# A graph layer on one core: the order of the table's chunks and the raw rows, and a first ring round worked off group by group

## The reference

```python
h = jnp.maximum(_layernorm(x, axis=-1), 0.0)                   # eps 1e-5
msg_in = jnp.concatenate([h[senders], edges], axis=-1)         # 320 values
agg = jax.ops.segment_sum(msg_in @ W_message, receivers, num_segments=12500)
g = _layer_norm(jax.nn.relu(agg) + h, ln_aggr_scale, ln_aggr_bias)
y = _relu_mlp_skip(g, [W0, W1, W2], [b0, b1, b2])              # three 256x256 layers
out = x + _layer_norm(h + y, ln_out_scale, ln_out_bias)
```

## Time and profile before

| | |
|---|---|
| median of 3 runs | 2189.6 us |
| profiled execution | 2189.61 us, span 2187.8 us |
| POOL busy | 1598.8 us, 73% |
| PE busy | 1700.8 us, 78% |
| DVE, ACT busy | 960.6 us, 393.6 us |
| first gather from the table | 133.80 us after the span's start |
| last gather issued | 2150.81 us |

### The profile page before, as it was taken

One profiled execution on the slowest core, in us unless ns is written; L12 is line 12 of the kernel. 1 busy time (PEld: TensorE's weight loads), 2 busy tenths in 40 slices (PEclk: granted clock), 3 DMA queues, 4 the chain that ended last, 5 costly groups with the idle time before them and its releaser, 6 DMA issues.

```text
span 2187.8 us, 31761 instructions
## 1 busy us (share of the span) xinstructions
PE 1700.8 (78%) x6728; PEld 1142.8 (52%) x6729; DVE 960.6 (44%) x4123; ACT 393.6 (18%) x1185; POOL 1598.8 (73%) x1672
## 2 busy tenths in 40 slices
PE   0149987888888788888788788878878878878887
PEld 0137765555555455555555555545545555545555
DVE  8956544344343434344343434434343434333345
ACT  2942111111111111111111111111111111111112
POOL 7547777777777777777777777777777777777772
PEclk9779999989888989999899899999998998999988
DMA  9966655555555555555555555555555555555542
GB/s 326 328 211 178 174 160 156 149 159 161 147 160 146 156 154 158 151 159 161 149 156 152 153 155 159 158 151 154 153 158 151 159 148 160 151 159 148 157 136 57
DMA packets 360746, 356.47 MB, mean 163 GB/s; under 512 B 250048, under 2 KB 303360, under 8 KB 360704
## 3 DMA queue, kind: packets, MB, share of 16 engines
q0 software_dynamic: 79872, 218.21, 34.6%
q1 hardware_dynamic: 221504, 83.44, 14.6%
q10 hardware_dynamic: 59328, 54.36, 7.8%
HBM read 329.39 MB, written 26.48 MB: 163 GB/s over the span
## 4 chain that ended last, share of the span: by engine, by line
POOL 66%; issue 21%; PE 4%; ACT 3%; DMA 3%; DVE 2%; POOLq 0%; SPq 0%; DVEq 0%
POOL ring L344 66%; PE acc_banks L489 2%; ACT xs L619 2%; DMA ring<-h_table,src_all 2%; ACT ring L619 1%; DMA xs<-x 1%; PE agg_bank L394 0%; PE agg_bank L399 0%; DVE x_stats L859 0%; PE y_bank L382 0%; PE z_bank L382 0%; DMA h_table<-xs 0%; PE acc_banks L394 0%; PE acc_banks L497 0%; ACT x_std L611 0%
## 5 line engine op out<-in xcount | busy, mean ns | idle before, releaser
L344 POOL DMA_INDIRECT ring<-h_table,src_all x1600 | 1530.8, 957 | 527.6 <-issue 484.4
L489 PE MATMUL acc_banks<-ring,onehot 128*128 128x320 f32 x3328 | 1147.9, 494 | 419.8 <-DMA ring<-h_table,src_all 341.9
L489 PEld LDWEIGHTS acc_banks<-ring,onehot 128*128 128x128 f32 x3328 | 673.4, 213 | 847.3 <-issue 689.2
L956 DVE TENSOR_SCALAR onehot<-iota,dst_rel 128x128 f32<-128x128 f32 x1664 | 354.4, 300 | 1157.5 <-PE acc_banks L489 1122.7
L533 ACT ACTIVATE uT<-z_bank,fp 128x128 f32<-128x128 f32 x196 | 79.1, 453 | 963.2 <-PE z_bank L388 959.2
L394 PE MATMUL agg_bank<-wm,ST 128*128 128x256 f32 (+1 forms) x582 | 164.2, 403 | 0.0
L394 PEld LDWEIGHTS agg_bank<-wm,ST 128*128 128x128 f32 (+1 forms) x582 | 105.6, 194 | 55.2 <-issue 35.1
L399 PE MATMUL agg_bank<-wl,u 128*128 128x256 f32 x392 | 111.6, 407 | 0.0
L549 ACT ACTIVATE std<-mv,eps 128x2 f32<-128x2 f32 x97 | 28.7, 296 | 448.9 <-DVE mv L677 448.9
L539 ACT ACTIVATE r_bank<-y_bank,fp 128x128 f32<-128x128 f32 x196 | 58.7, 337 | 280.3 <-PE y_bank L382 280.3
L382 PEld LDWEIGHTS y_bank<-u,wl 128*128 128x128 f32 x784 | 102.9, 191 | 5.3 <-issue 0.3
(11 more groups left out here) (166 smaller groups left out, 1032.0 us busy)
## 6 DMA issues: line engine op xcount, KB each, us to landing
ring<-edges SPq DMA_DIRECT2D x208, 256.0 KB, 3.6
ring<-h_table,src_all POOLq DMA_INDIRECT x1600, 2.8
xs<-x SPq DMA_DIRECT2D x14, 896.0 KB, 10.0
h_table<-xs SPq DMA_DIRECT2D x14, 896.0 KB, 5.0
h_in<-h_table ACTq DMA_DIRECT2D x98, 128.0 KB, 2.4
visit_rows<-h_table ACTq DMA_DIRECT2D x98, 128.0 KB
visit_rows<-x ACTq DMA_DIRECT2D x98, 128.0 KB
out<-o ACTq DMA_DIRECT2D x93, 128.0 KB
```

Source lines behind the costliest of these rows:

```text
L344: nc.gpsimd.indirect_dma_start(out=ring[:, g % RG * G + j, 0:D], out_offset=None, in_=rows, in_offset=bass.IndirectOffsetOnAxis(ap=src_all ...
L489: return nc.tensor.matmul(acc_of(at), onehot[:, (k % OG) * G + j, :], ring[:, k * G + j, :], start=False, stop=True, skip_group_check=True)
L956: op = nc.vector.tensor_scalar(onehot[:, ((k + AHEAD) % OG) * G + j, :], iota[:, :], dst_rel[:, bass.ds((g + AHEAD) * G + j, 1)], None, AL ...
```

## The change

UNITS now is chunks 0 to 12, raw 0, chunk 13, raw 1 to raw 7. The first FIRST = 16 units (up to raw 1) are taken before the loop over groups. In `x_moments(u)` the aggregation of unit u-1 now comes behind the first statistics of unit u, and `x_stats` has two halves. Raw 2 to raw 7 are taken one at a time, between the first round's groups: on DVE `x_moments(16+k)` and then group k, on ACT `x_root` and `x_to_h` of raw k+1 and then group k's visit, if it has one. DVE's and ACT's first round is written out; DVE's loop starts at round 1 and ACT's loop at the visit that follows the first round. A second pass over the edges (for unusual edge lists, not taken here) now stands under an `If` on DVE. The first round's edge loads go out with chunks 6 to 13, not 0 to 7.

The key setup is shared out: ACT copies `blk` and `dst_f` and makes both range checks with a sum over the row (`accum_out`); DVE's two row-wide reductions, the product `blk * ok` and the cast of `blk` go; the remaining parts stand behind units 0, 1, 3, 4, 5 and 6, and the first one-hots in front of units 14 and 15.

```diff
-    UNITS = []
-    for n in range(NX):
-        UNITS.append(("chunk", n))
-        if 3 <= n < 3 + RG:
-            UNITS.append(("raw", n - 3))
-    UNITS += [("raw", k) for k in range(max(NX - 3, 0), RG)]
+
+
+    UNITS = [("chunk", n) for n in range(NX)]
+    UNITS.insert(NX - 1, ("raw", 0))
+    UNITS += [("raw", k) for k in range(1, RG)]
+    FIRST = NX + 2
...
-                if n < RG:
-                    load_edges(n, 0, n + 1)
+                if n >= NX - RG:
+                    load_edges(n - NX + RG, 0, n - NX + RG + 1)
                 if n >= 1 and n - 1 + XS < NX:
                     sp.wait_ge(h_stored[(n - 1) % XS], 16 * ((n - 1) // XS + 1))
                     load_x(n - 1 + XS)
...
+            act.wait_ge(lasts_ready, 1)
+            nc.scalar.activation(blk[:, 1:T + 1], last_i[:, :], ACT.Copy).then_inc(blocks_ready, 1)
             x_root(0)
-            for u in range(1, len(UNITS)):
+            act.wait_ge(dst_in, 16)
+            nc.scalar.activation(dst_f[:, :], dst_i[:, :], ACT.Copy).then_inc(dst_ready, 1)
+            for u in range(1, FIRST - 1):
                 x_root(u)
+                if u == 2:
+
+                    act.wait_ge(rel_ready, 1)
+                    nc.scalar.activation(rel[:, :], rel[:, :], ACT.Relu, bias=highest[:, 0:1],
+                                         accum_out=wrong[:, 0:1]).then_inc(wrong_ready, 1)
+                    nc.scalar.activation(below[:, :], below[:, :], ACT.Relu, scale=-1.0,
+                                         accum_out=wrong[:, 1:2]).then_inc(wrong_ready, 1)
                 x_to_h(u - 1)
-            x_to_h(len(UNITS) - 1)
+            x_to_h(FIRST - 2)
             act.wait_ge(params_in, PARAMS)
...
-            sel_reg = registers(nc.scalar, 1)
+            regs = registers(nc.scalar, W - AT)
+            before = [nc.scalar.alloc_register(f"before{k}") for k in range(4)]
 
             def row(b):
                 return out_blocks[:, bass.ds(b, 1), :].rearrange("p b d -> p (b d)")
 
-            for n in range(LAG):
-                sel = numbers(nc.scalar, sel_reg, visit_sel, n, 1)[0]
-                act_visit(act, n, sel, max(n - 1, 0), max(n - 4, 0), dump)
-            with nc.scalar.Fori(LAG, NB - 1) as n:
-                sel = numbers(nc.scalar, sel_reg, visit_sel, n, 1)[0]
-                act_visit(act, n, sel, n - 1, n - 4, row(n - LAG))
-            sel = numbers(nc.scalar, sel_reg, visit_sel, NB - 1, 1)[0]
+            def visit(n, sel):
+
+                load_at, late_at, store_at = (floored(nc.scalar, to, n, -lag) for to, lag in zip(before, (1, 4, LAG)))
+                act_visit(act, n, sel, load_at, late_at, row(store_at))
+
+
+            for k in range(RG):
+                if k + 1 < RG:
+                    x_root(FIRST - 1 + k)
+                    x_to_h(FIRST - 1 + k)
+                _, sel, closes, _ = numbers(nc.scalar, regs, steer_flat, k * W + AT, G - 1, 1, T)
+                n = floored(nc.scalar, before[3], regs[VISIT - AT])
+                with nc.scalar.If(closes > 0):
+                    visit(n, sel)
+                    nc.scalar.nop()
+            nc.scalar.load(regs[0:1], steer_flat[0:1, RG * W + VISIT:RG * W + VISIT + 1])
+            visited = floored(nc.scalar, before[3], regs[0])
+            with nc.scalar.Fori(visited, NB - 1) as n:
+                sel = numbers(nc.scalar, regs[1:2], visit_sel, n, 1)[0]
+                visit(n, sel)
+            sel = numbers(nc.scalar, regs[1:2], visit_sel, NB - 1, 1)[0]
             act_end(act, sel, row(NB - 1 - LAG))
...
+            def x_aggregate(u):
+                dve.wait_ge(x_stats_ready, u + 1)
+                if u >= 2:
+                    dve.wait_ge(x_norm_ready, u - 1)
+                for k in range(XB if UNITS[u][0] == "chunk" else G):
+                    op = nc.vector.bn_aggr(x_mv[:, u % 2, k, :], x_stats[:, u % 2, k, :])
+                op.then_inc(x_moments_ready, 1)
...
-                if u >= 1:
-                    dve.wait_ge(x_moments_ready, u)
+                if u >= 2:
+                    dve.wait_ge(x_moments_ready, u - 1)
+                left = [] if u == 0 else list(range(5))
                 for k in range(count):
                     rows_at = xs[:, n % XS, k, :] if kind == "chunk" else ring[:, n * G + k, 0:D]
-                    op = nc.vector.bn_stats(x_stats[:, k, :], rows_at)
+                    op = nc.vector.bn_stats(x_stats[:, u % 2, k, :], rows_at)
                     if k == count - 1:
                         op.then_inc(x_stats_ready, 1)
-                    if u >= 1 and k < 5:
-                        x_scale(u - 1, k)
-                dve.wait_ge(x_stats_ready, u + 1)
-                if u >= 2:
-                    dve.wait_ge(x_norm_ready, u - 1)
-                for k in range(count):
-                    op = nc.vector.bn_aggr(x_mv[:, u % 2, k, :], x_stats[:, k, :])
-                op.then_inc(x_moments_ready, 1)
-
...
+            def check_keys():
+                dve.wait_ge(blocks_ready, 1)
+                dve.wait_ge(dst_ready, 1)
+                nc.vector.scalar_tensor_tensor(rel[:, :], blk[:, 1:T + 1], -float(P), dst_f[:, :], ALU.mult, ALU.add)
+                nc.vector.scalar_tensor_tensor(below[:, :], blk[:, 0:T], -float(P), dst_f[:, :], ALU.mult, ALU.add).then_inc(rel_ready, 1)
+                step(nc.vector.tensor_tensor(spans[:, :], blk[:, G:T + 1:G], blk[:, 0:T:G], ALU.subtract))
+                step(nc.vector.tensor_reduce(widest[:, :], spans[:, :], AX.X, ALU.max))
+                nc.vector.tensor_scalar(narrow[:, :], widest[:, :], 1.0, None, ALU.is_le)
+
+            def relative_keys():
+                dve.wait_ge(wrong_counted, 1)
+                step(nc.vector.tensor_reduce(n_wrong[:, :], n_wrong_at, AX.X, ALU.add))
+                step(nc.vector.tensor_scalar(ok[:, :], n_wrong[:, :], 0.0, narrow[:, 0:1], ALU.is_equal, ALU.mult))
+                nc.vector.tensor_copy(ok_i[:, :], ok[:, :])
+                step(nc.vector.tensor_scalar(per_block[:, :], ok[:, :], -float(P), None, ALU.mult))
+                step(nc.vector.scalar_tensor_tensor(dst_rel[:, 0:T], blk[:, 1:T + 1], per_block[:, 0:1], dst_f[:, :], ALU.mult, ALU.add))
+                nc.vector.tensor_scalar(dst_rel[:, T:T + AHEAD * G], dst_rel[:, 0:AHEAD * G], -float(P), None, ALU.add).then_inc(keys_ready, 1)
...
+            parts = {0: cast_iotas, 1: check_keys, 3: relative_keys, 4: closing_places, 5: steering, 6: second_layer}
+            for u in range(FIRST):
+                if u == FIRST - 2:
+                    for late in range(u, len(parts) + 1):
+                        parts[late]()
+                    first_onehots(0)
+                elif u == FIRST - 1:
+                    first_onehots(1)
                 x_moments(u)
-            for k in range(5):
-                x_scale(len(UNITS) - 1, k)
+                if u < FIRST - 2 and u in parts:
+                    parts[u]()
+                if u == 0:
+                    shift_lasts()
 
             dve.wait_ge(tables, 1)
             dve.wait_ge(rows_ready, 1)
...
+            for k in range(RG):
+                if k + 2 < RG:
+                    x_moments(FIRST + k)
+                elif k + 2 == RG:
+                    x_finish()
+                group(0, 0, k)
+            with nc.Fori(1, ROUNDS, engines=[mybir.EngineType.DVE], hint_back_edge=True) as i:
+                for k in range(RG):
+                    group(0, i, k)
```

More of the change, by code:

```diff
@@ L313, in _ @@
                     load_x(n - 1 + XS)
-            for k in range(NX, RG):
+            for k in range(RG - min(NX, RG)):
                 load_edges(k, 0, k + 1)
@@ L903, in _ @@
-            step(nc.vector.scalar_tensor_tensor(dst_rel[:, 0:T], blk[:, 1:T + 1], -float(P), dst_f[:, :], ALU.mult, ALU.add))
-            nc.vector.tensor_scalar(dst_rel[:, T:T + AHEAD * G], dst_rel[:, 0:AHEAD * G], -float(P), None, ALU.add).then_inc(keys_ready, 1)
-            x_moments(3)
+                    if u >= 1 and k == 0:
+                        x_aggregate(u - 1)
+                    if k >= 2 and left:
+                        x_scale(u - 1, left.pop(0))
+                for k in left:
+                    x_scale(u - 1, k)
```

175 lines of the change are left out of this document (91 added, 84 removed).

## The result

The changed kernel took 2198.58 us in the median (2196.56 to 2202.18, 5 runs), the kernel before 2188.51 (2185.91 to 2190.01, 5 runs) on the same chip: a ratio of 1.0046, 95% interval [1.0035, 1.0057]. It is slower by 10 us. The forecast was 2207, with a range from 2190 to 2218. The profiled run took 2198.69, with a span of 2196.9.

What follows compares the result with a forecast made beforehand. POOL's gathers were taken to bound the kernel, through their start and the timely freeing of slots. 2189.6 - 5.7 (earlier table) + 22.6 (first-round waits) + 0.5 (jump at the end) = 2207.0 us, range 2190 to 2218.

Steps and rivals of the forecast that it cites:

- The mechanism: First round: raw rows in turn with visits free POOL's slots late, four times, adding 22.6 us of waiting for PE.
- Half clock: Rival, first round: PE throttled throughout, z to freed slot 12.0 us, waits 35 instead of 22.6, time 2219; chance 15%.
- term 1: Program start up to the stored table: first table gather at 128.1 instead of 133.80, a gain of 5.7 us.
- the end: Kernel's end: DVE's new jump over the second pass costs between 0 and 2 us, taken as 0.5.

Runs made afterwards that it cites:

- k1: The changed kernel run again unaltered, on a chip where the kernel before took 2188.43 us: 2196.77 us, ratio 1.0037.
- p1: The changed kernel with two small iotas on POOL before every gather, on a 2188 us chip: 2396.93 us, 1.0948 of the kernel before.
- e4: The changed kernel with 20 idle matmuls on zeros before PE's wait for z in first-round visits; slow chip: 2946.92 us, 1.0054 of the kernel before.
- e2: The changed kernel with ACT's six DMAs issued by SP and the broadcast rows copied earlier; slow chip: 2949.15 us, 1.0053 of the kernel before.
- e3: The changed kernel with all raw rows normalised in one block behind the chunks, before the first visit; slow chip: 2943.34 us, 1.0033 of the kernel before.
- e1: The changed kernel with all raw groups again normalised in turns with the chunks, before the first gather; slow chip: 2936.76 us, 1.0008 of the kernel before.
- f2: The changed kernel with raw 0 to 5 in turns with chunks 5 to 10, SP issuing the six DMAs; slow chip: 2972.38 us, 0.9996 of the kernel before.
- p2: The changed kernel with the old raw-row order and two small iotas before each gather; slow chip: 2570.57 us, 0.8730 of the kernel before.

## Why the prediction was right, point by point

**The mechanism stood.** Slots 1, 2, 4 and 6 were forecast late, to be freed 14.7, 34.2, 59.4 and 83.2 us after the first gather, with waits of 4.6, 9.4, 5.0 and 3.6; they were refilled at 15.2, 34.4, 57.6 and 82.4, with waits of 5.4, 9.4, 3.4 and 4.7. All waits for PE rose by 23.6 us, forecast 22.6. The places are the forecast's merit; that the sizes agree so well is luck, since two errors cancel. z of the first visit was done at +23.5 (148.14) instead of +26.3: some 1.5 us of it because raw groups take ACT 6.1 us and not 6.8, 0.9 because the one-hots begin without the 0.7 us of issue, which the traces don't show there. And PE needed 10.8 us from z to the slot (148.19 to 159.03) instead of 7.9. Over the three visits PE took 10.8, 8.3 and 10.6 us, 6.0 more than the forecast's 23.7, and the steps of ACT and DVE between them 6.8 less.

**Half clock was half a rival.** Visits 1 and 3 came near it (9.86 and 9.65 us from z to the tiles, where the warm visits have 5.56), the second lies between (7.30). Together they are 10.1 us longer than warm ones; the first visit of the kernel before was 1.7 longer itself. That rival asked for 12.0 from z to the slot throughout, 36.0 for three, and a sum of 35: the three took 29.7, and z came earlier than in the forecast. Its 2219 us also lay 1 us above the range that was said to hold it. The Trainium skill, "TensorE: Matmul & The Clock Gate" (What's actually happening), has the throttled state as the default that activity lifts; the windows agree (0.73 at 125 to 150 us, 0.95 at 200 to 250). How much of the 10.1 reaches the end wasn't measured on a 2188 us chip.

**The term that was mis-sized is term 1.** The table was 9.16 us sooner (9.8 in k1), not 5.7. ACT's wide operations took 1.59, 1.57, 1.67 and 1.57 us, not 1.4, plus 0.19 and 0.18 for two accumulators; even so the store of chunk 2 went out at 43.04, forecast 44.2. Chunks 5 to 12 started at 45.70, 52.79, 58.79, 66.23, 72.52, 82.15, 90.43 and 97.47 (forecast 49.3, 55.8, 63.3, 69.8, 77.5, 85.3, 93.0, 99.7): the pace was nearly right, 7.4 us a chunk (forecast 7.2), and the row began 3.6 early. Chunk 5's load went out at 38.75 and not 40.3, and landed within 7.0 us, taken as 9. At chunk 12 2.2 us were left, at the last chunk's rows (119.4 against 122.6) 3.2. Loads of 9.5 us and five buffers now bound the chunks, and DVE's 26.8 us of waiting for them show it; so emptying ACT by half (16.32 of 33.00 us busy) gave 9 us and not the 38 of the raw units moved away. That the last chunk had to wait for them is what the forecast had said.

**The sum.** 2207 less 3.5 (table), plus 1.0 (first round), less 1.3 (the end came 0.75 sooner instead of 0.5 later), less 4.5: POOL's 1600 gathers took 1528.1 and 482.6 us instead of 1530.8 and 484.4. That gives 2198.7, the profiled run. The last item isn't the change's: in k1 these were 1532.5 and 482.1, and its profiled run took 2204.1. So the gain at the start is 9.2 to 9.8, the loss 23.6 to 24.3, and the net by the mechanism some 14.5 us. The medians lie only 10.1 and 8.3 us over those of before; these 4 to 6 us stay unexplained (the gathers' 4.5 us is of that size, but only in the first profile).

**What is shown and what is argued.** Shown on 2188 us chips: the waits, their places, what ACT and DVE did in them, and by p1 that the freeing chain sets them. That the order of the raw rows causes them follows there from reading the trace; undoing the order bears it out, but only on slow chips. On one of them the old order took 10.2 us less than e4 and 12.4 less than e2, although its first table gather was 17 to 18 us later: its first round is 24 to 29 us shorter. For the rival that the first round written out costs by itself nothing speaks: the old order keeps it and stands at 0.9966 to 1.0008 of before, on slow chips, and in the changed kernel's profile start, gathers, waits for PE and end account for the whole difference. A run of the old order at 2188 us, for which 2179 to 2187 us was expected, was not had.

## What to carry to other kernels

Work that is moved from a place where its engine is busy to one where it is free is not free when another engine's list has it behind something else: here DVE was idle for 21 and ACT for 26 of the 50 us from 150 on, and POOL still lost 23.6 us, because on both engines' lists raw rows stood ahead of visits and visits ahead of raw rows, and a visit waits across three engines. e3 shows on a slow chip that one block of raw rows ahead of the first visit still loses to the old order. Ask of each moved step which item stands ahead of it on every engine's list, and when that item ends; a walk with a clock through those lists, from rows of the kernel before, gave the four waits to within 2 us, though partly by errors that cancelled. And where the buffers and transfers bound a stage, taking half the work off its busiest engine returns only what the transfers leave.

## What the runs showed of the hardware that was not expected

**The same kernel takes 2188 us on some chips and 2934 to 2988 on others.** The granted clock is lower there (0.79 to 0.82 in the mean, 0.91 here), but from 200 to 2100 us the visits' `wm` matmuls take 412 ns in e1 and 406 in the changed kernel, and a gather takes 957 ns there, 955 here; nor are transfers slower: the chunk loads land in 7.3 us in e1's page, 9.5 in the changed kernel's. What is longer is the waiting. In e1 the groups are:

```profile
L357 POOL DMA_INDIRECT ring<-h_table,src_all x1600 | 1530.6, 957 | 1241.6 <-PE acc_banks L502 685.3 <-issue 457.9 <-DMA h_table<-xs 78.6
...
L546 ACT ACTIVATE uT<-z_bank,fp 128x128 f32<-128x128 f32 x196 | 78.9, 453 | 1755.7 <-remote 1710.3
```

Its timeline around 1000 us, PE, POOL and ACT:

```profile
1002.50 0.38 PE L401 MATMUL z_bank<-ident,z 128*128 128x128 f32 x2
...
1013.78 0.95 POOL L357 DMA_INDIRECT ring<-h_table,src_all  x1 [0.30 <-issue]
...
1017.44 0.46 ACT L546 ACTIVATE uT<-z_bank,fp 128x128 f32<-128x128 f32 x1 [18.53 <-remote]
```

PE transposes z at 1002.5 to 1002.9, and ACT, which waits for nothing else, goes on at 1017.44, 2.7 us after the end of the last gather of a burst of 16 that began at 994.86. The hold isn't there from the burst's start: z, done on DVE at 1001.3, still reaches PE at 1002.5. In the trace's record of semaphore updates those of PE, five of them over 4 us of matmuls, all arrive between 1017.4 and 1017.7, while updates by landing DMAs arrive all the time between. At the program's start it looks the same: the 64 raw gathers go out from 7.2 to 93 us, and in f2 DVE stands between small operations until 98. From both (16 gathers in 22.7 us, 64 in 91) I estimated 1.40 to 1.42 us a gather on a path that gathers and updates would share, against the 1.25 at which POOL issues. That there is such a path is a guess.

p2 tests it: more work on POOL, 1.38 us a gather, and the time **falls** to 0.873 of the kernel before on that chip [0.871, 0.8749], where the same iotas cost 9.5% on a 2188 us chip (p1, with the changed order; without iotas the old order had 0.9966 to 1.0008). POOL there, and PE and ACT around 1010 us:

```profile
L365 POOL DMA_INDIRECT ring<-h_table,src_all x1600 | 1520.0, 950 | 244.0 <-issue 223.6
...
L362 POOL IOTA pace<- 128x32 int32 x3328 | 454.3, 174 | 202.8 <-remote 126.8
```

```profile
1009.54 1.06 PE L403 MATMUL z_bank<-uT,wl 128*128 128x128 f32 x8
...
1016.85 0.60 ACT L560 ACTIVATE r_bank<-z_bank,fp 128x128 f32<-128x128 f32 x2 [5.80 <-remote]
```

POOL's waits before a group now stand at its iotas: 126.8 us marked `remote`, where e1 had 685.3 for PE. The first gather came at 151.43 instead of 171 to 173, expected 130 to 150. That gathers issued faster than some path takes them hold up the engines' semaphore updates is so far borne out, and the rival (PE or the transfers slower by themselves, 2900 or more) is out. Two details missed: 2400 to 2550 us was expected, 2570.57 measured, with two groups every 23.5 us, 1.47 us a gather; and no hold over 3 us was expected, while around 1010 us ACT goes on 6.2 us after PE was done (1010.6). What sets that pace, and why some chips have it and others not, no run here tells.
